# Squares of the third tile through the device's memory, values five halves behind, and the ends of attention rearranged

## What is computed

```
ffn:  8 experts of hidden size 176, the two best by sigmoid(x @ gate.T) + bias,
      h = square(relu(x_routed @ up_e.T)), y = h @ down_e.T   (bf16)
      plus a shared expert in fp32: square(relu(x @ sup.T)) @ sdown.T
attention: q = x @ Wq.T + bq; probs = softmax(q @ keys.T / sqrt(128))  over 4096 keys
           out = (probs @ values) @ Wo.T + bo
```

## Time and profile before

| | |
|---|---|
| time, median of 3 runs | 693.62 us (691.54 to 698.07) |
| the profiled execution | 697.09 us, span 695.3 us |
| busy: PE, DVE, ACT, POOL | 89%, 77%, 68%, 56% of the span |
| DMA of SP's queue | 60.57 MB, 34.8% of 16 engines |
| first feed-forward, first product to last | 17.3 to 120.8 us |
| attention, first scores to last values | 120.5 to 601.9 us |
| second feed-forward | from 605.1 us |

### The profile page before, as it was taken

The page is one execution under the profiler, slowest core; times in us unless marked ns, Lnnn a source line. Parts: engine busy times, 40 slices in busy tenths (PEclk is TensorE's granted clock), DMA queues, the critical chain, the costliest instruction groups (busy, mean ns, idle before and its releaser), DMA issues.

```text
span 695.3 us, 9149 instructions
## 1 busy us (share of the span) xinstructions
PE 617.1 (89%) x2768; PEld 429.7 (62%) x2768; DVE 533.2 (77%) x952; ACT 469.5 (68%) x773; POOL 392.7 (56%) x386
## 2 busy tenths in 40 slices
PE   3898979657998998999999999999999858699997
PEld 2544434535876776877777777777777646454542
DVE  3798876866977977888887897896797645188885
ACT  2477979335776776777776777776776644178886
POOL 4755512024765865867766677686687687542200
PEclk9799999988999999999999999999999988899999
DMA  7002010065364453553653644635526530000001
GB/s 286 2 30 62 30 61 0 8 160 124 73 155 95 115 133 86 139 131 77 156 117 74 152 108 104 145 93 127 133 65 149 120 81 0 1 6 26 31 18 44
DMA packets 37092, 61.17 MB, mean 88 GB/s; under 512 B 9051, under 2 KB 9651, under 8 KB 36915
## 3 DMA queue, kind: packets, MB, share of 16 engines
q1 hardware_dynamic: 36755, 60.57, 34.8%
q10 hardware_dynamic: 288, 0.01, 0.0%
HBM read 8.12 MB, written 2.10 MB: 15 GB/s over the span
## 4 chain that ended last, share of the span: by engine, by line
PE 40%; SPq 22%; DVE 14%; issue 11%; POOL 6%; ACT 6%; DMA 1%; ACTq 0%; DVEq 0%; POOLq 0%
SPq L323 22%; PE banks L1021 4%; POOL p_lo L423 4%; PE banks L1030 3%; PE banks L1138 3%; PE banks L1179 3%; PE banks L1140 3%; PE banks L1139 3%; PE banks L1178 3%; PE banks L1180 3%; DVE probsT L810 3%; PE banks L986 3%; DVE bank_max L909 3%; DVE E L904 2%; PE banks L1037 2%
## 5 line engine op out<-in xcount | busy, mean ns | idle before, releaser
L423 POOL TENSOR_TENSOR p_lo<-probsT,p_hi 128x768 fp32r<-128x768 f32 x128 | 235.4, 1842 | 136.3 <-ACT p_hi L629 135.6
L909 DVE TENSOR_REDUCE bank_max<-banks 128x1 f32<-128x1024 f32 x128 | 155.8, 1217 | 36.3 <-PE banks L1140 35.7
L629 ACT ACTIVATE p_hi<-probsT 128x768 fp32r<-128x768 f32 x128 | 107.9, 843 | 30.1 <-issue 27.2
L1138 PE MATMUL banks<-kv_lo,q_parts 128*128 128x512 f32 x256 | 112.5, 440 | 13.6 <-ACT E L647 10.3
L810 DVE SCALAR_TENSOR_TENSOR probsT<-banks,E 128x1024 bf16<-128x1024 f32 x80 | 95.5, 1219 | 35.3 <-PE banks L1021 31.6
L904 DVE STREAM_TRANSPOSE E<-E 128x1024 f32<-128x1024 f32 x96 | 118.4, 1234 | 4.2 <-ACT E L647 4.2
L647 ACT ACTIVATE E<-banks,neg_max 128x1024 f32<-128x1024 f32 x96 | 106.8, 1113 | 20.7 <-DVE neg_max L915 13.4
L531 ACT ACTIVATE probsT<-probsT 128x1024 bf16<-128x1024 bf16 x96 | 92.2, 980 | 31.8 <-DVE probsT L810 22.9
L1178 PE MATMUL banks<-p_hi,kv_lo 128*128 128x512 f32 x256 | 109.3, 427 | 3.9 <-POOL p_lo L423 3.9
L621 ACT ACTIVATE p_hi<-banks 128x256 fp32r<-128x256 f32 x128 | 49.0, 383 | 82.1 <-PE banks L1157 82.0
L1179 PE MATMUL banks<-p_lo,kv_hi 128*128 128x512 f32 x256 | 103.7, 405 | 0.0
(11 more groups left out here) (101 smaller groups left out, 874.8 us busy)
## 6 DMA issues: line engine op xcount, KB each, us to landing
probsT<-E SPq DMA_DIRECT2D x256, 128.0 KB, 2.4
probsT<-E SPq DMA_DIRECT2D x256, 64.0 KB, 2.0
E<-in_keys_values SPq DMA_DIRECT2D x8, 512.0 KB, 3.4
out<-X SPq DMA_DIRECT2D x8, 256.0 KB, 2.1
X<-in_x SPq DMA_DIRECT2D x1, 1280.0 KB, 8.8
X<-in_x SPq DMA_DIRECT2D x3, 256.0 KB, 5.2
probsT<-in_wup SPq DMA_DIRECT2D x1, 704.0 KB, 6.7
probsT<-in_wdown SPq DMA_DIRECT2D x1, 704.0 KB, 6.2
```

Of the source, the lines that this page charges most:

```text
L423: pool.tensor_tensor(moved_part(p_lo, ring), moved_pair(ring // UP, ring % UP), moved_part(p_hi, ring).bitcast(fp32), ALU.subtract).then_i ...
L629: act.activation(moved_part(p_hi, ring), moved_pair(ring // UP, ring % UP), ACT.Copy).then_inc(moved_hi_done, 1)
L909: dve.tensor_reduce(bank_max[:, i % 2, h:h + 1], score_pair(u, i, h).rearrange("p b n -> p (b n)"), AX.X, ALU.max).then_inc(bank_max_done, 1)
L1138: pe.matmul(bank, qh, kl, start=True, stop=False)
```

## The change

- The values come five halves behind the exponentials' unit instead of six (LAG), in unit 0 two halves behind (FIRST_LAG). The steps that hang on a pair move with it; the q work goes to halves 3 and 4, project_out to half 6.
- In units 1 to 14 the second batch is one write of tile 2's squares to a buffer in the device's memory (spill), a wait for it on SP, and four reads back, one to each strip of 32 partitions of probsT. Tile 2's place in E2 is free once the write has landed.
- Units 0 and 15 move only tiles 0 and 1 (moved_tiles); tiles 2 and 3 are both transposed by PE. In unit 0 half of the sixteen transfers are issued by ACT.
- At the end of attention DVE, not POOL, normalizes group 2, casts three groups, spreads the weights and adds the last two blocks; the last block is projected and copied inside group 0 of the second feed-forward.
- In the first feed-forward kv_hi is formed by POOL, group 0 is normalized by DVE, group 0's weights are turned ahead of the shared product, and the first two scores stand among the last down products.

```diff
-LAG = 12
-FILL_HALF = HALVES + LAG // 2 - 2
-VALUE_HALF = HALVES + LAG // 2
-PROJECT_HALF = LAG // 2 + 1
-Q_HALF = 5
+LAG = 5
+FIRST_LAG = 2
+PROJECT_HALF = LAG + 1
+ADD_HALF = LAG
+Q_HALF = 3
...
+        spill = nc.dram_tensor("spill", [2, P, QUADS * N], fp32, kind="Internal").ap()
...
+        def moved_tiles(w):
+
+            return 2 if w in (0, LAST) else MOVED
...
+        def moves(k, units):
+
+            return 16 * (QUADS * QUADS * units if k == 0 else QUADS * max(0, min(units, LAST) - 1))
+
+        def spills(u):
+
+            return 16 * len([w for w in range(1, LAST) if w <= u and w % 2 == u % 2])
+
+        def squares_of(units):
+            return 2 * sum(moved_tiles(w) for w in range(units))
+
+        def move_strip(eng, u, k, b, i):
+
+            first, count = BATCHES[k]
+            target = probsT[b * SQ:(b + 1) * SQ, u % 2, :, :, :].rearrange(
+                "p (t i) c q -> p i t (c q)", t=MOVED)[:, i, first:first + count, :]
+            eng.dma_start(target, E2[i * SQ:(i + 1) * SQ, first:first + count, b, :]).then_inc(moved[k], 16)
+
+        def pairs_until(H):
+
+            first = 2 * HALVES + FIRST_LAG
+            return max(0, min(H - HALVES - FIRST_LAG, UP) if H <= first else
+                       min(max(H - HALVES - LAG, UP), UNITS * UP))
+
+        def pair_at(H):
+
+            return pairs_until(H) if pairs_until(H + 1) > pairs_until(H) else None
+
+        def projection_at(H):
+
+            w = H // HALVES - 2
+            if w < 0 or w >= LAST:
+                return None
+            return w if H % HALVES == (FIRST_LAG if w == 0 else LAG) + 1 else None
...
+                    if first >= moved_tiles(u):
+                        continue
+                    sp.wait_ge(squares_done, squares_of(u) + 2 * (first + count))
+                    if k == 1:
+                        wait(sp, moved[1], moves(1, u - 1))
+                        sp.dma_start(spill[u % 2], E2[:, first, :, :].rearrange("p b n -> p (b n)")
+                                     ).then_inc(spilled[u % 2], 16)
+                        sp.wait_ge(spilled[u % 2], spills(u))
+                        for b in range(QUADS):
+                            sp.dma_start(probsT[b * SQ:(b + 1) * SQ, u % 2, first * QUADS:, :, :].rearrange(
+                                "p i c q -> p i (c q)"), spill[u % 2][:, b * N:(b + 1) * N].rearrange(
+                                "(i p) n -> p i n", i=QUADS)).then_inc(moved[1], 16)
+                        continue
+
+                    for b in range(QUADS // 2 if u == 0 else QUADS):
                         for i in range(QUADS):
-                            target = probsT[b * SQ:(b + 1) * SQ, u % 2, :, :, :].rearrange(
-                                "p (t i) c q -> p i t (c q)", t=MOVED)[:, i, first:first + count, :]
-                            sp.dma_start(target, E2[i * SQ:(i + 1) * SQ, first:first + count, b, :]
-                                         ).then_inc(moved[k], 16)
+                            move_strip(sp, u, k, b, i)
...
+                        pool.wait_ge(kv_loaded[i % 2], (i // 2 + 1) * 16)
+                        pool.tensor_copy(kv_hi[:, i, :], kv_stage[:, i % 2, :]).then_inc(kv_hi_done, 1)
...
-                    ring = pair_at(u * HALVES + h, VALUE_HALF - 4)
+                    ring = pair_at(u * HALVES + h + 4)
...
-                    if u == LAST + 1 and h == 0:
-                        cast_xT(SECOND_LN, GROUPS, 0)
-                    if u == LAST + 1 and h == 2:
-                        normalize(SECOND_LN + 2, 2)
-                    if u == LAST + 1 and h == 3:
-                        cast_xT(SECOND_LN + 1, GROUPS + 1, 1)
+                    if u == LAST + 1 and h == 4:
                         inverse_deviation(SECOND_LN + 3)
-                    if u == LAST + 1 and h == 5:
-                        cast_xT(SECOND_LN + 2, GROUPS + 2, 2)
-                    if u == LAST + 2 and h == 1:
-                        spread_weights(GROUPS)
...
                     if f == 0 and i == 0:
+                        copy_wbc(0, xT_bank)
                         shared_relu(G)
-                        copy_wbc(0, xT_bank)
                         copy_xT(2, 2, 2, xT_bank)
                         exp_logits(2, gate_bank[:, 0:GT * E])
                     square(G, 0)
                     if f or i:
                         shared_relu(G)
+                    if f and i == 0:
+                        copy_y(LAST)
...
-                    if f == 0:
-                        split_kv(i)
...
-                if i < MOVED:
-                    if h == 0:
-                        wait(act, moved[batch_of(i)], moves(u))
-                        if u == 0 and i == MOVED - 1:
-                            act.wait_ge(kv_lo_done, KV)
+                if i < MOVED and h == 0:
+                    if i < BATCHES[1][0]:
+                        wait(act, moved[0], moves(0, u))
+                    elif u >= 2:
+                        act.wait_ge(spilled[(u - 1) % 2], spills(u - 1))
+                    if u == 1 and i == MOVED - 1:
+                        act.wait_ge(kv_lo_done, KV)
+                if i < moved_tiles(u):
...
-                    if 2 <= u and h == LAG // 2 - 2:
-                        copy_oT(u - 2)
-                    ring = pair_at(H + 1, FILL_HALF)
+                    w = projection_at(H + 3)
+                    if w is not None:
+                        copy_oT(w)
+                    if u == LAST + 2 and h == LAG - 2:
+                        copy_oT(LAST)
+                    if u == LAST + 1 and h == 3:
+                        early_copy(1, banks[:, 1, :])
+                    if u == LAST + 1 and h == 5:
+                        exp_logits(GROUPS + 1, early_logits(1))
+                        early_copy(2, banks[:, 0, :])
+                    if u == LAST + 1 and h == 6:
+                        exp_logits(GROUPS + 2, early_logits(2))
+                    if u == LAST + 2 and h == 3:
+                        copy_wbc(GROUPS, banks[:, 2, :])
+
+                    ring = pair_at(H + 3)
                     if ring is not None:
                         own_high(ring)
                     if u < UNITS:
                         exponentials(u, h // 2, h % 2)
+                    if u == 0 and h == 5:
+                        act.wait_ge(z_done, GROUPS)
+                        act.wait_ge(down_done, GROUPS * SLOTS)
+                        act.wait_ge(squares_done, squares_of(1))
+                        for b in range(QUADS // 2, QUADS):
+                            for i in range(QUADS):
+                                move_strip(act, 0, 0, b, i)
...
+            def normalize_first():
+
+                dve.wait_ge(rstd_done, 1)
+                for t in range(GT):
+                    last = dve.tensor_scalar(xn[:, t, :], X[:, t, :], neg_mean[:, t:t + 1], rstd[:, t:t + 1],
+                                             ALU.add, ALU.mult)
+                last.then_inc(normalized, 1)
...
+            def add_last_block(w):
+
+                dve.wait_ge(y_copied, w + 1)
+                dve.wait_ge(merge_b, 4 * GROUPS)
+                dve.wait_ge(bias_added, GROUPS)
+                dve.wait_ge(block_added, w)
+                for t in range(GT):
+                    tile = X[:, (GROUPS - 1) * GT + t, :]
+                    last = dve.scalar_tensor_tensor(tile, y[:, t, :], share[:, w % 2, t:t + 1], tile,
+                                                    ALU.mult, ALU.add)
+                last.then_inc(block_added, 1)
...
+                        if g == 0:
+                            normalize_first()
...
+                    if u == LAST + 1 and h == 3:
+                        normalize_early(SECOND_LN + 2, 2)
+                    if u == LAST + 1 and 4 <= h < 7:
+                        cast_early(h - 4)
+                    if u == LAST + 1 and h >= 6:
+                        for k in range(6 * (h - 6), 6 * (h - 5)):
                             route_group(k, GROUPS)
+                    if u == LAST + 2 and h == 0:
+                        for k in range(12, STEPS + 1):
+                            route_group(k, GROUPS)
+                        spread_early()
+                    if u == LAST + 2 and h == 1:
+                        add_last_block(LAST - 1)
...
+                    if f == 0 and i == 0:
+                        pe.wait_ge(xT_copied, 2)
+                        transpose_weights(0, xT_bank)
...
                     if f and i == 0:
-
-                        pe.wait_ge(oT_copied, UNITS)
-                        pe.wait_ge(y_copied, UNITS)
-                    up(G, 1)
+                        pe.wait_ge(p_lo_done, UNITS * UP)
+                        project_out(LAST)
...
-                for k in range(3, SLOTS):
-                    down(base + GROUPS - 1, k)
+
+                down_last = base + GROUPS - 1
                 if f == 0:
```

(59 more changed lines are left out.)

74 lines of the change are left out of this document (38 added, 36 removed).

## The result

The changed kernel takes 754.4 us (median of 4 runs, 753.6 to 757.8) against 694.8 of the kernel before in the same session; the ratio is 1.087, interval 1.080 to 1.093. The forecast was 691, with 662 to 710 as its range. The profiled execution took 757.8, its span 756.0, against 697.1 and 695.3 before.

The account below looks back on a forecast made before the run. The loop of moved squares was taken to bound attention's middle units. Terms -5, -2, +19, -15 and +0.5 sum to -2.5, span 695.3 to 692.8; adjusted to the runs' median, about 691 us, range 662 to 710.

Parts of the forecast that it names:

- What bounds: Attention's middle units: a loop from first batch through landing and ACT's release to the next unit's first batch sets the period.
- D: Middle units: time from first batch's start until moved squares land and ACT goes on; 21.2 us forecast, range 19.2 to 22.5.
- Release to next start: Middle units: from ACT's release to the next unit's first batch, 4.1 us before, forecast 7.5 (7.1 to 8.0).
- The steady units: Attention's middle: period 28.7 us, some 1.35 us longer in each of 14 periods, +19 us (-8 to +45).
- Unit 0 and the start of unit 1: Start of attention: two tiles moved and ACT issuing half the transfers, earlier landing mostly used up; -2 us (-6 to +3).
- Before attention: First feed-forward: work moved between engines, weights turned and first scores formed earlier; -5 us (-9 to 0).
- The end: From unit 15's first batch to the second feed-forward's first product: 44 us against 58.7, counted as -15 (-8 to -20).
- The second feed-forward: After attention: it takes in the last projection and its copies, +0.5 us.
- Rival (c): Middle units: longer stalls let PE's clock fall if gaps pass some 2.8 us; +28 us, 715 to 720; chance 0.13.
- Rival (b): Middle units: reads at full rate or lost half largely absorbed, period near 26.9; 666 us (658 to 680); chance 0.33.
- Rival (d): End of attention: work moved to DVE lies on own_low's path, -5 instead of -15; 701 us; chance 0.12.
- the bound of 30.5 us a unit: Middle units: upper end of the period, with 22.5 us to ACT's release and 8.0 to the next start; +45 us.

Follow-up runs that it names:

- best3: Changed kernel with six halves, strip transfers, SP alone issuing, three tiles moved in unit 0 and its values three halves behind; 703.4 us, ratio 1.013.
- best: Like best3, but unit 0's values six halves behind and no PE wait for unit 0's copy before unit 1's first transposes; 686.2 us, ratio 0.987.
- sp_all6: Changed kernel with six halves, the third tile moved in strips, and SP issuing all of unit 0's transfers; 692.4 us, ratio 0.996.
- fill: Changed kernel with PE forming one half's scores three times in units 2 to 14, results the same; 754.7 us, ratio 1.083.
- wide: Changed kernel with the four reads going to all 128 partitions, so tile 2's share of the output differs; 719.8 us, ratio 1.031.

## Why the prediction was wrong

**What bounds**: right. The loop of D and release sets the period wherever three tiles are moved. That the first high part comes a half sooner and that the exponential after the next is then the one waited for was right too, and it is the cause.

**Release to next start, 7.5 us (7.1 and 8.0)**: too low, the first of three steps that failed. Measured 9.0: about 8 without the q work, about 10 with it. I added 3.4, the distance of two exponentials in the trace of before; the turn of the second I left 1.8 behind it, as there. In fact the exponentials are 2.6 us apart in the one kind and 5.2 in the other, where the q copy and a pair of values stand between, and the turn comes 2.5 to 3.0 behind, as the maximum ahead of it waits for a PE that has only just been released. I took the rows of a flowing schedule for one that restarts.

**D, 21.2 us**: the second step that failed, by 2.2. The write was right (4.2 forecast, 4.45 from its issue to the first read's). The reads were 7.6 instead of 6.6. Their four landings, 1.21 us apart, make 4.8 us of bytes where I had 4.5, so the strips' rate was the right row; the rest is 2.8 us, where I had a fixed part of 2.1 from loads over all partitions. The 1.3 us between the first and the fourth issue are hidden behind the landings. The first batch up to the write took 11.3 instead of 10.3. Its sixteen issues, 0.64 us each in the earlier trace rows, took 11.65 in the row above, because single ones are long. SP's issues of strips in units 1 to 15, duration in ns min/median/max:

```profile
L312 SPq DMA_DIRECT2D probsT<-E x240: 585/597/2142, 167.0 to 631.3; - x120
```

Eleven of the 240 took 1.35 to 2.14 us. Such issues stand in the trace of before too (eleven of 512, 1.2 to 2.05 us), and my sum of medians left them out. In units 8 and 14 SP also waited 0.4 and 2.2 us for tile 2's turn. Why single issues are long, and why more of them fall into the first batch here, is open; with six halves the mean is 10.7. So D rose to 23.4 where it was to fall, above the upper end of 22.5.

**The steady units, +19**: measured +71.6. 1.5 us of release and 2.2 of D in each of 14 periods are 52 of the 53 us that are missing. Both misses were in the terms that bind at full weight, and my case with both at their worst ended at +45.

**Unit 0 and the start of unit 1, -2**: measured +8, the third step that failed. I looked at the landing (which was sooner: first high part 11.4 us after the start, against 22.1) and not at what the earlier values push back. best3 and best show it. ACT's eight issues took 8.4 us, where I had 5.1; sp_all6 shows that this matters little.

**Before attention, -5**: measured -4.3. **The end, 44 us**: measured 44.0; but 4 to 9 of the 14.7 us won are the short lag's, and with six halves the end takes 48 to 52. That the end hit to 0.1 us is in part luck, two misses that cancel: ACT's first own_high of unit 15 comes at 639.5, 17.8 us after the first batch where I had 6 + 10, and the rest takes 26.2 where I had 20 + 8, with the eight own_high 3.1 us apart and own_low at 0.69 us (0.7 forecast). **The second feed-forward, +0.5**: 0.1.

**Rival (c)**, the clock: its sign came, 87 us at the lower level, its gaps too (4.31 us where 2.8 was the bound), but not as the price: fill halves it, and the time stays. **Rival (b)** fell to the strips' rate; by wide the faster reads would have been worth 35 us and not enough. **Rival (d)** did not occur.

What happened, the lost half at its full price, was in my text as the bound of 30.5 us a unit and got no chance of its own; the measured 32.4 lie even above that bound.

## What to carry to other kernels

Where a loop of transfers and hand-overs sets the period, every step between a release and the next issue counts in full, however idle the engines are; a shorter pipeline lag saves at most its half once at the end (4 to 9 us here, nothing where the last landing bound) and costs it in each turn. Price such a stretch by following the queues in order from a restart, with every instruction ahead of the waited-for one, not by the spacing of a row from a schedule that flows. Test the lag alone first: it was one constant, and undoing it turned +8.7% into nothing; with the good parts kept, and the start of attention and the strips as before, it became -1.3%.

## What the runs showed of the hardware

Two queues that issue at once each slow down: SP's and ACT's eight strips of unit 0 took 8.36 us side by side (1.04 us each, 0.52 per transfer over both), against 0.64 us on SP alone: the second queue brings a fifth, not a half. The last strip landed 11.4 us after the first issue, against 12.2 by SP alone in sp_all6.

```profile
132.74 8.36 SPq L312 DMA_DIRECT2D probsT<-E  x8
```

Four overlapping reads of 256 KB from the device's memory: in 32 partitions the first lands in 3.9 us and each further one 1.2 later (217 GB/s), in 128 partitions the first in 3.2 and each further one 0.75 later (350 GB/s). A strip transfer costs SP 0.60 us to issue by the median, but 11 of 240 issues took 1.35 to 2.14 in after. Writing 1 MiB there and reading it back costs 4.45 + 7.6 = 12 us, as much as sixteen transfers within the core with their last landing (16 x 0.64 + 2.0).
